# Self-attention of a decoder kernel: the softmax exponentials are divided by their sums on GpSimd ahead of the transposing, in place of dividing the output of the value matmuls

## The chip, the cores and the metric

The kernel runs on one core of a Trainium2 chip. The metric is the device time of one execution in microseconds; lower is better. The core's engines are TensorE (PE in the profile; its weight loads are listed as PEld), VectorE (DVE), ScalarE (ACT), GpSimd (POOL) and SyncE (SP, which issues DMAs here).

## The reference, cut to what matters

The whole program is a two-layer decoder; only the first layer's self-attention changes. It has 2 sequences of 1024 tokens, 16 heads of 64 columns, a relative-position bias, and computes, for each head,

```
scores = q @ k.T * 64**-0.5 + bias[q - k]     # 1024 x 1024
p      = exp(scores - max) / sum(exp(scores - max))
out    = p @ v                                # 1024 x 64
```

Dividing each row of the exponentials by its sum, or dividing the matching row of `exp @ v`, gives the same result up to rounding.

## The kernel before, in words

`self_attention` is written by hand, one instruction stream for each engine, with semaphores between them. A **block** is a pair of heads of one sequence (16 blocks). A block has 8 **iterations**, one for each 128 queries: n runs from 0 to 127. An iteration has two **stages**, one for each head of the pair, numbered st = 2n and 2n+1. I call them the first and the second stage of the iteration. Two iterations make a **group** g of 256 queries (64 groups), whose outputs leave together.

What one stage does, in order of the data:

1. PE `scores` (L578) makes 128 x 1024 scores in two PSUM banks; both stages of the iteration come out of one set of 12 matmuls.
2. DVE `biased` (L730) adds the bias strip, writes 128 x 1024 values to `sm` (a ring of 4 slots) and their extreme to `mn`.
3. ACT `exps` (L663) takes the exponentials in place and puts the row sums in `rsum`.
4. PE `transposed` (L591) waits for `exps` and transposes the eight 128 x 128 pieces into two PSUM banks, which ACT (L668) and DVE (L737), both called `emptied`, copy to `pT`.
5. PE `values` (L606) multiplies the transposed exponentials of a whole group by V, half of it in each iteration of the next group, into one half of bank 6 (64 output columns of each head on the partitions, 256 queries along the bank).

The division runs once a group: DVE `inverted` (L742) takes the reciprocals of 4 columns of sums; PE (L613), behind the second half of `values`, spreads them with 4 small matmuls against the identity into the other half of bank 6; ACT `spread_inverse` (L674) copies that half to `inv`; DVE `normed` (L748) multiplies it with the outputs into `o`; SP stores `o` (L553).

GpSimd has no work in this part of the program. `project` (L629, L634, L637) are the projections for the block after this one, one unit at the end of each iteration n < 120: in each run of 8 iterations four units for k and q, then four for v. The last 8 iterations have none. `split` prepares weights, 7 times.

The order of the work on each engine is the order of the code. On PE, iteration n is: scores(n+1), transposed(n, 0), half of values, transposed(n, 1), project.

Of the kernel before, what the change touches and what calls it, by code (L numbers as in the profile page):

```python
# [24 lines left out]
ALU = mybir.AluOpType  # L25
ACT = mybir.ActivationFunctionType
AX = mybir.AxisListType

P = 128
# [453 lines left out]
def self_attention(nc, A, S, K, psum):  # L483
# [6 lines left out]
    with ExitStack() as ctx:  # L490
# [14 lines left out]
        sm = sb("sm", [P, RING, T])  # L505
        mn, rsum = sb("mn", [P, SUMS]), sb("rsum", [P, SUMS])
        pT = sb("pT", [P, 2, 2, KT, GQ])
        inv = sb("inv", [P, GQ])
        o = sb("o", [P, 2, GQ])


# [22 lines left out]
        with turn(nc, sig) as block:  # L534
# [29 lines left out]
            @block.tensor  # L564
            def _(pe):
                def scores(n):
                    _, b, qt = tiles[n]
                    if n % KT == 0:
                        pe.wait_ge(sig("proj_out"), NU * (n // KT) + 4)
                    if n:  # L570
                        pe.wait_ge(sig("biased"), 2 * n)
                    q = slice(qt * P, (qt + 1) * P)
                    for c in range(2):
                        k = slice(c * CH, (c + 1) * CH)
                        for i, (qq, kk) in enumerate(((QH, KH), (QL, KH), (QH, KL))):
                            for hl in range(2):
                                rows = slice(hl * DH, (hl + 1) * DH)
                                last = pe.matmul(scores_banks(hl)[:, c, :], qq[rows, b, q], kk[rows, b, k],  # L578
                                                 start=i == 0, stop=i == 2)
                                if c == 1 and i == 2:  # L580
                                    last.then_inc(sig("scores"), 1)

                def transposed(n, hl):
                    st = 2 * n + hl
                    pe.wait_ge(sig("exps"), st + 1)
                    for j, emptied in enumerate(("pT_act", "pT_dve")):
                        if st:
                            pe.wait_ge(sig(emptied), st)
                        for k in range(4):
                            kt = 4 * j + k  # L590
                            last = pe.transpose(psum[:, 4 + j, k * P:(k + 1) * P], sm[:, st % RING, kt * P:(kt + 1) * P], ident[:, :])  # L591
                        last.then_inc(sig("p_ps"), 1)

                def values(g, half):

                    _, b, _ = tiles[2 * g]
                    if half == 0:
                        pe.wait_ge(sig("pT_act"), 4 * (g + 1))
                        pe.wait_ge(sig("pT_dve"), 4 * (g + 1))
                        pe.wait_ge(sig("proj_out"), NU * (2 * g // KT + 1))  # L600
                        if g:
                            pe.wait_ge(sig("o_out"), g)
                    for kt in range(half * KT // 2, (half + 1) * KT // 2):
                        for hl in range(2):
                            rows = slice(hl * DH, (hl + 1) * DH)
                            pe.matmul(bank_o[rows, 0:GQ], V[:, b, kt, rows], pT[:, g % 2, hl, kt, :],  # L606
                                      start=kt == 0, stop=kt == KT - 1)
                    if half:
                        pe.wait_ge(sig("inverse"), g + 1)
                        for t in range(2):  # L610
                            for hl in range(2):
                                at = (4 * g + 2 * t + hl) % SUMS
                                last = pe.matmul(bank_o[hl * DH:(hl + 1) * DH, GQ + t * P:GQ + (t + 1) * P],  # L613
                                                 rsum[:, at:at + 1].broadcast_to([P, DH]), ident[:, :], start=True, stop=True)
                        last.then_inc(sig("o_ps"), 1)

                def project(u):
                    pair, b, what, c = units[u]
                    bank, W = unit_bank(u), Ws[pair % 2]
                    if u >= NU:  # L620
                        pe.wait_ge(sig("proj_out"), u)
                    if u % (2 * NU) == 0 and pair:
                        pe.wait_ge(sig("w_lo"), pair)
                    terms = passes(KC)
                    tok = slice(b * T + c * CH, b * T + (c + 1) * CH)
                    if what in "qk":
                        col = slice(0, P) if what == "q" else slice(P, 2 * P)
                        for i, (ws, hs, k) in enumerate(terms):
                            last = pe.matmul(bank, W[:, ws, k, col], hT[hs][:, k, tok], start=i == 0, stop=i == len(terms) - 1)  # L629
                    else:  # L630
                        for t in range(2):
                            tile = slice(b * T + (2 * c + t) * P, b * T + (2 * c + t + 1) * P)
                            for k in range(KC):
                                pe.matmul(bank[:, t * 2 * P:(t + 1) * 2 * P].rearrange("p (s n) -> p s n", s=2), hT[0][:, k, tile],  # L634
                                          W[:, :, k, 2 * P:3 * P], start=k == 0, stop=False)
                            for k in range(KC):
                                last = pe.matmul(bank[:, t * 2 * P:t * 2 * P + P], hT[1][:, k, tile], W[:, 0, k, 2 * P:3 * P],  # L637
                                                 start=False, stop=k == KC - 1)
                    last.then_inc(sig("proj_ps"), 1)

                for u in range(NU):
                    project(u)
                scores(0)
                for n in range(NI):
                    if n + 1 < NI:
                        scores(n + 1)
                    transposed(n, 0)
                    if n > 1:
                        values(n // 2 - 1, n % 2)
                    transposed(n, 1)  # L650
                    if NU + n < len(units):
                        project(NU + n)
                values(NG - 1, 0)
                values(NG - 1, 1)

            @block.scalar
            def _(a):
                def exps(st):
                    a.wait_ge(sig("biased"), st + 1)
                    at = st % SUMS  # L660
                    if st >= SUMS:
                        a.wait_ge(sig("o_ps"), st // 4 - 2)
                    a.activation(sm[:, st % RING, :], sm[:, st % RING, :], ACT.Exp, scale=-1.0,  # L663
                                 bias=mn[:, at:at + 1], accum_out=rsum[:, at:at + 1]).then_inc(sig("exps"), 1)

# [1 line left out]
                    a.wait_ge(sig("p_ps"), 2 * st + 1)  # L667
                    a.activation(probs(st, 0), psum[:, 4, :].rearrange("p (k q) -> p k q", k=4), ACT.Copy).then_inc(sig("pT_act"), 1)  # L668

                def spread_inverse(g):  # L670
                    a.wait_ge(sig("o_ps"), g + 1)
                    if g:
                        a.wait_ge(sig("o_out"), g)
                    a.activation(inv[:, :], bank_o[:, GQ:2 * GQ], ACT.Copy).then_inc(sig("inv_out"), 1)  # L674

                def project(u):

# [24 lines left out]
                exps(1)  # L702
                for n in range(NI):
                    if n % 2 == 0 and n > 2:
                        spread_inverse(n // 2 - 2)
                    emptied(2 * n)
                    if n + 1 < NI:
                        exps(2 * n + 2)
# [4 lines left out]
                        project(NU + n)  # L713
                    if n % (2 * KT) == 2 and n // (2 * KT) + 1 < HP:
                        split(n // (2 * KT) + 1)
                spread_inverse(NG - 2)
                spread_inverse(NG - 1)

            @block.vector
            def _(v):  # L720
# [15 lines left out]
                    v.wait_ge(sig("p_ps"), 2 * st + 2)  # L736
                    v.tensor_copy(probs(st, 1), psum[:, 5, :].rearrange("p (k q) -> p k q", k=4)).then_inc(sig("pT_dve"), 1)  # L737

                def inverted(g):
                    v.wait_ge(sig("exps"), 4 * (g + 1))  # L740
                    part = rsum[:, 4 * g % SUMS:4 * g % SUMS + 4]
                    v.reciprocal(part, part).then_inc(sig("inverse"), 1)  # L742

                def normed(g):
                    v.wait_ge(sig("inv_out"), g + 1)
                    if g >= 2:
                        v.wait_ge(sig(f"st{g % 2}"), 16 * (g // 2))
                    v.tensor_tensor(o[:, g % 2, :], bank_o[:, 0:GQ], inv[:, :], ALU.mult).then_inc(sig("o_out"), 1)  # L748

                def project(u):  # L750

# [21 lines left out]
                    project(u)  # L773
                biased(0)
                biased(1)
                for n in range(NI):
                    if n % 2 == 0 and n > 2:
                        normed(n // 2 - 2)
                    if n and NU + n - 1 < len(units):
                        project(NU + n - 1)  # L780
                    if n + 1 < NI:
# [2 lines left out]
                    if n + 1 < NI:  # L784
                        biased(2 * n + 3)
                    emptied(2 * n + 1)
                    if n % 2:
                        inverted(n // 2)
                    if n % (2 * KT) == 3 and n // (2 * KT) + 1 < HP:
                        split(n // (2 * KT) + 1)  # L790
                normed(NG - 2)
                normed(NG - 1)


def start(nc, have, rows, weights, zeros=None):
# [1503 lines left out]
```

## Time and profile before

| | us |
|---|---|
| median of 3 runs (2507.12 to 2510.59) | 2510.52 |
| the profiled execution | 2507.76 |
| its span in the profile | 2506.0 |
| PE busy over the span | 2126.9 |
| DVE busy | 1527.2 |
| ACT busy | 1034.9 |
| POOL busy | 608.1 |

The self-attention loop lies between about 60 and 935 us of the span. Busy time of PE overlaps its own weight loads, and ends of matmuls are modelled, so the spacing of starts tells more than the durations. A row of a timeline gives the start, the duration, the engine, the line, the operation, its tiles and, in brackets, the idle time of the engine before it and what ended it.

### The profile page before, as it was taken

The numbers are of one execution on the slowest core, as the hardware profiler recorded it, in microseconds if no ns is written. First come the engines' busy times: TensorE is split into PE (matmuls) and PEld (weight loads), VectorE is DVE, ScalarE is ACT, GpSimd is POOL, SyncE is SP. The second block draws the span as 40 slices with busy tenths as digits, with TensorE's granted clock in tenths as the row PEclk, the third lists the DMA queues.
The fourth block names the chain that finished last, engine by engine and source line by source line (L and its number), as shares of the span: only waits on it lengthen the run. The fifth ranks groups of instructions, "written<-read, shape, count | busy, mean of one in ns | idle before, by whom it ended". The sixth has DMA issues, their size and how long they took to land. (4 is left out here: it accounts for less than half of the span.)

```text
span 2506.0 us, 48610 instructions
## 1 busy us (share of the span) xinstructions
PE 2126.9 (85%) x19484; PEld 1756.7 (70%) x19484; DVE 1527.2 (61%) x3236; ACT 1034.9 (41%) x2036; POOL 608.1 (24%) x596
## 2 busy tenths in 40 slices
PE   5999999999999985788876488999658989866885
PEld 4777777777777764676765488888648888865673
DVE  5666666666666651689897455554445454434885
ACT  3666666566665650333432232332223332222442
POOL 1000000000000001466666223323222333323552
PEclk8999999999999997899987699999879999988997
DMA  6001101010110004021100210000021000003000
GB/s 233 14 16 43 43 16 43 16 49 12 47 43 10 12 14 169 27 70 36 36 18 9 97 48 10 10 14 10 5 110 44 15 14 27 10 10 110 10 9 18
DMA packets 59968, 96.79 MB, mean 39 GB/s; under 512 B 7720, under 2 KB 50480, under 8 KB 57392
## 3 DMA queue, kind: packets, MB, share of 16 engines
q1 hardware_dynamic: 52608, 69.49, 8.6%
q10 hardware_dynamic: 7136, 24.19, 2.5%
q8 instruction: 156, 2.56, 0.4%
q14 instruction: 68, 0.56, 0.1%
HBM read 70.45 MB, written 23.20 MB: 37 GB/s over the span
## 5 line engine op out<-in xcount | busy, mean ns | idle before, releaser
L730 DVE CUSTOM_DVE_ANT_0 a_sm<-psum,a_strip 128x1024 f32<-128x1024 f32 x256 | 311.8, 1218 | 34.6 <-PE psum L578 34.4
L663 ACT ACTIVATE a_sm<-a_sm,a_mn 128x1024 f32<-128x1024 f32 x256 | 293.4, 1146 | 29.7 <-DVE a_mn L730 29.6
L591 PE MATMUL psum<-ident,a_sm 128*128 128x128 f32 x2048 | 280.0, 280 | 1.1 <-ACT a_pT L668 1.0
L591 PEld LDWEIGHTS psum<-ident,a_sm 128*128 128x128 f32 x2048 | 219.5, 141 | 83.9 <-issue 58.5
L668 ACT ACTIVATE a_pT<-psum 128x512 f32<-128x512 f32 x256 | 152.9, 597 | 303.5 <-PE psum L591 303.5
L737 DVE COPY a_pT<-psum 128x512 f32<-128x512 f32 x256 | 176.3, 689 | 131.5 <-PE psum L591 131.5
L606 PE MATMUL psum<-a_pT,a_V 128*64 128x256 f32 x2048 | 249.0, 385 | 1.3 <-DVE a_o L748 1.3
L1130 POOL TENSOR_TENSOR b_x<-b_x,b_bo_a 128x512 f32<-128x512 f32 x8 | 10.2, 1280 | 937.6 <-POOLq L798 937.6
L606 PEld LDWEIGHTS psum<-a_pT,a_V 128*64 128x64 f32 x2048 | 136.2, 136 | 77.5 <-issue 22.3
L578 PE MATMUL psum<-a_KH,a_QH 64*128 64x512 f32 x512 | 115.1, 445 | 2.5 <-DVE a_mn L730 2.5
L1020 PE MATMUL psum<-b_w,b_act_hi 128*128 128x256 f32 x256 | 64.7, 337 | 56.3 <-POOL b_act_lo L1118 56.3
L1126 POOL TENSOR_TENSOR b_gs<-b_gate,b_sg 128x512 f32<-128x512 f32 x64 | 96.7, 1510 | 28.5 <-ACT b_sg L1042 27.9
L578 PE MATMUL psum<-a_KL,a_QH 64*128 64x512 f32 x512 | 102.4, 395 | 0.0
L578 PE MATMUL psum<-a_KH,a_QL 64*128 64x512 f32 x512 | 101.7, 392 | 0.0
L225 PE MATMUL psum<-sa_eT,sa_wqkv 128*128 128x256 f32 x768 | 94.5, 283 | 2.8 <-DVE sa_eT L1719 2.7
L225 PE MATMUL psum<-la_eT,la_wqkv 128*128 128x256 f32 x768 | 95.1, 284 | 1.7 <-DVE la_eT L1719 1.7
L225 PEld LDWEIGHTS psum<-sa_eT,sa_wqkv 128*128 128x128 f32 x768 | 92.9, 192 | 3.5 <-DVE sa_eT L1719 3.4
L225 PEld LDWEIGHTS psum<-la_eT,la_wqkv 128*128 128x128 f32 x768 | 93.4, 193 | 2.5 <-DVE la_eT L1719 2.3
L1118 POOL TENSOR_TENSOR b_act_lo<-b_act,b_act_hi 128x512 fp32r<-128x512 f32 x64 | 83.3, 1302 | 48.2 <-ACT b_act_hi L1049 48.2
L1020 PEld LDWEIGHTS psum<-b_w,b_act_hi 128*128 128x128 f32 x256 | 44.9, 213 | 69.9 <-POOL b_act_lo L1118 69.1
L629 PE MATMUL psum<-a_hT_hi,a_W 128*128 128x512 f32 x256 | 76.5, 421 | 12.2 <-PEq L72 12.2
L206 PE MATMUL psum<-b_wo,b_oT 128*128 128x256 f32 x256 | 58.5, 388 | 24.2 <-PEq L798 24.2
(381 smaller groups left out, 4675.4 us busy)
## 6 DMA issues: line engine op xcount, KB each, us to landing
a_strip<-table SPq DMA_DIRECT2D x16, 960.0 KB, 6.7
oT<-a_o SPq DMA_DIRECT2D x64, 128.0 KB, 1.9
b_oT<-oT SPq DMA_DIRECT2D x8, 1024.0 KB, 5.4
a_raw<-in_a_wqkv SPq DMA_DIRECT2D x7, 384.0 KB, 3.2
s_x<-in_x_rev SPq DMA_DIRECT2D x4, 512.0 KB, 8.1
vb<-s_zero SPq DMA_DIRECT2D x8, 256.0 KB, 2.9
b_x<-in_x SPq DMA_DIRECT2D x8, 256.0 KB, 5.5
b_vb<-vb SPq DMA_DIRECT2D x8, 256.0 KB, 6.0
```

The lines of the kernel that those rows point to most:

```text
L225: last = pe.matmul(bank[:, i * CP:(i + 1) * CP], weight[:, wp, k, m * P:(m + 1) * P], cols[:, cp, k, :], start=n == 0, stop=n == len(terms ...
L578: last = pe.matmul(scores_banks(hl)[:, c, :], qq[rows, b, q], kk[rows, b, k], start=i == 0, stop=i == 2)
L591: last = pe.transpose(psum[:, 4 + j, k * P:(k + 1) * P], sm[:, st % RING, kt * P:(kt + 1) * P], ident[:, :])
L606: pe.matmul(bank_o[rows, 0:GQ], V[:, b, kt, rows], pT[:, g % 2, hl, kt, :], start=kt == 0, stop=kt == KT - 1)
L629: last = pe.matmul(bank, W[:, ws, k, col], hT[hs][:, k, tok], start=i == 0, stop=i == len(terms) - 1)
L663: a.activation(sm[:, st % RING, :], sm[:, st % RING, :], ACT.Exp, scale=-1.0, bias=mn[:, at:at + 1], accum_out=rsum[:, at:at + 1]).then_in ...
L668: a.activation(probs(st, 0), psum[:, 4, :].rearrange("p (k q) -> p k q", k=4), ACT.Copy).then_inc(sig("pT_act"), 1)
L730: v.tensor_tensor_reduce(out=sm[:, st % RING, :], in0=scores_banks(hl).rearrange("p c n -> p (c n)"), in1=strip[:, pair % 2, hl, qt * P:qt ...
L737: v.tensor_copy(probs(st, 1), psum[:, 5, :].rearrange("p (k q) -> p k q", k=4)).then_inc(sig("pT_dve"), 1)
L1020: last = pe.matmul(bank[:, t * D:(t + 1) * D], half[:, e % 2, k, t * P:(t + 1) * P], w2[:, e, k, :], start=i == 0, stop=i == len(parts) - 1)
L1118: g.tensor_tensor(act_lo[:, e % 2, :, :], act[:, e % 2, :, :], act_hi[:, e % 2, :, :].bitcast(F32), ALU.subtract).then_inc(sig("m_lo"), 1)
L1126: g.tensor_tensor(gs[:, n % ER, :, :], gate[:, n % ER, :, :], sg[:, n % ER, :, :], ALU.mult).then_inc(sig("m_gs"), 1)
```

## The change

The reciprocals are now taken stage by stage (`inverted(st)` on DVE, one column each), GpSimd multiplies the 128 x 1024 exponentials of the stage with them in place, and `transposed` waits for that product (`scaled`) instead of for `exps`. The four spreading matmuls, the tile `inv` and DVE's `normed` are gone; ACT's `stored` copies the finished outputs from bank 6 to `o`. ACT's reuse of a column of `rsum` now waits for `scaled` instead of `o_ps`.

```diff
@@ tensor
                 def transposed(n, hl):
                     st = 2 * n + hl
-                    pe.wait_ge(sig("exps"), st + 1)
+                    pe.wait_ge(sig("scaled"), st + 1)
@@ values(g, half)
                     if half:
-                        pe.wait_ge(sig("inverse"), g + 1)
-                        for t in range(2):
-                            for hl in range(2):
-                                at = (4 * g + 2 * t + hl) % SUMS
-                                last = pe.matmul(bank_o[hl * DH:(hl + 1) * DH, GQ + t * P:GQ + (t + 1) * P],
-                                                 rsum[:, at:at + 1].broadcast_to([P, DH]), ident[:, :], start=True, stop=True)
                         last.then_inc(sig("o_ps"), 1)
@@ scalar
-                        a.wait_ge(sig("o_ps"), st // 4 - 2)
+                        a.wait_ge(sig("scaled"), st - SUMS + 1)
-                def spread_inverse(g):
+                def stored(g):
                     a.wait_ge(sig("o_ps"), g + 1)
-                    if g:
-                        a.wait_ge(sig("o_out"), g)
-                    a.activation(inv[:, :], bank_o[:, GQ:2 * GQ], ACT.Copy).then_inc(sig("inv_out"), 1)
+                    if g >= 2:
+                        a.wait_ge(sig(f"st{g % 2}"), 16 * (g // 2))
+                    a.activation(o[:, g % 2, :], bank_o[:, 0:GQ], ACT.Copy).then_inc(sig("o_out"), 1)
@@ gpsimd (new)
+                for st in range(2 * NI):
+                    at = st % SUMS
+                    g.wait_ge(sig("inverse"), st + 1)
+                    g.tensor_scalar(sm[:, st % RING, :], sm[:, st % RING, :], rsum[:, at:at + 1], None, ALU.mult).then_inc(sig("scaled"), 1)
@@ vector
-                def inverted(g):
-                    v.wait_ge(sig("exps"), 4 * (g + 1))
-                    part = rsum[:, 4 * g % SUMS:4 * g % SUMS + 4]
-                    v.reciprocal(part, part).then_inc(sig("inverse"), 1)
-                def normed(g):
-                    v.wait_ge(sig("inv_out"), g + 1)
-                    if g >= 2:
-                        v.wait_ge(sig(f"st{g % 2}"), 16 * (g // 2))
-                    v.tensor_tensor(o[:, g % 2, :], bank_o[:, 0:GQ], inv[:, :], ALU.mult).then_inc(sig("o_out"), 1)
+                def inverted(st):
+                    v.wait_ge(sig("exps"), st + 1)
+                    at = st % SUMS
+                    v.reciprocal(rsum[:, at:at + 1], rsum[:, at:at + 1]).then_inc(sig("inverse"), 1)
@@ vector, the loop over n
+                inverted(0)
                 for n in range(NI):
-                    if n % 2 == 0 and n > 2:
-                        normed(n // 2 - 2)
+                    inverted(2 * n + 1)
                     if n and NU + n - 1 < len(units):
                         project(NU + n - 1)
                     if n + 1 < NI:
                         biased(2 * n + 2)
                     emptied(2 * n)
                     if n + 1 < NI:
                         biased(2 * n + 3)
                     emptied(2 * n + 1)
-                    if n % 2:
-                        inverted(n // 2)
+                    if n + 1 < NI:
+                        inverted(2 * n + 2)
```

On PE, in the middle of the program where the projections are for v, this stood before: the transposes of a first stage (L591), the second half of values (L606), the spreading matmuls (L613), the transposes of the second stage, then the projection (L634, L637) and the scores of the iteration after next (L578).

```order
299 L591 MATMUL psum<-ident,a_sm 128x128 x8
300 L606 MATMUL psum<-a_pT,a_V 64x256 x8
301 L613 MATMUL psum<-ident,a_rsum 64x128 x4
302 L591 MATMUL psum<-ident,a_sm 128x128 x8
303 L634 MATMUL psum<-a_W1,a_hT_hi 128x256 x2
304 L637 MATMUL psum<-a_W1,a_hT_lo 128x128 x2
305 L634 MATMUL psum<-a_W1,a_hT_hi 128x256 x2
306 L637 MATMUL psum<-a_W1,a_hT_lo 128x128 x2
```

The same place of the change (transposes are L590 there, values L605, the projection L627 and L630):

```order
290 L590 MATMUL psum<-ident,a_sm 128x128 x8
291 L605 MATMUL psum<-a_pT,a_V 64x256 x8
292 L590 MATMUL psum<-ident,a_sm 128x128 x8
293 L627 MATMUL psum<-a_W1,a_hT_hi 128x256 x2
294 L630 MATMUL psum<-a_W1,a_hT_lo 128x128 x2
295 L627 MATMUL psum<-a_W1,a_hT_hi 128x256 x2
296 L630 MATMUL psum<-a_W1,a_hT_lo 128x128 x2
```

Only the four spreading matmuls are gone; nothing else moved on PE. What stands between the transposes of a second stage and those of the next first stage is still one projection and one set of scores.

On DVE, with the semaphores that each row waits for, an iteration's end stood like this before (L730 is `biased`, L737 the copy that empties a bank of transposes, L742 the reciprocal of four columns, L748 `normed`, L764 the second half of a projection):

```order
307 L730 ISA a_sm,a_mn<-psum,a_strip 128x1024 [waits a_ld_strip0,a_scores,a_p_ps]
308 L730 ISA a_mn 128x1
309 L737 COPY a_pT<-psum 128x4x128 [waits a_p_ps]
310 L742 RECIPROCAL a_rsum<-a_rsum 128x4 [waits a_exps]
311 L748 TENSOR_TENSOR a_o<-psum,a_inv 128x256 [waits a_st0,a_inv_out]
312 L764 TENSOR_TENSOR a_V<-a_V,psum 128x256 [waits a_proj_hi]
313 L730 ISA a_sm,a_mn<-psum,a_strip 128x1024 [waits a_scores,a_p_ps]
```

The same place of the change:

```order
312 L730 ISA a_sm,a_mn<-psum,a_strip 128x1024 [waits a_ld_strip0,a_scores,a_p_ps]
313 L730 ISA a_mn 128x1
314 L737 COPY a_pT<-psum 128x4x128 [waits a_p_ps]
315 L742 RECIPROCAL a_rsum<-a_rsum 128x1 [waits a_exps] x2
316 L758 TENSOR_TENSOR a_V<-a_V,psum 128x256 [waits a_proj_hi]
```

The two reciprocals stand side by side: the first is that of the next iteration's first stage, behind the copy that empties the bank of this iteration's second stage; the second is that of the next iteration's second stage. On POOL there are 256 new rows `TENSOR_SCALAR a_sm<-a_sm,a_rsum 128x1024` in a line, each waiting for its reciprocal.

## Rows read from the trace of the kernel before

**Rows 1.** Busy time by engine, 400 to 600 us (PE, PEld, DVE, ACT, POOL; clock, DMA)
```profile
400.00:600.00 200.00, 200.00 (x1604) 147.70 (x1602) 129.68 (x237) 122.07 (x221) 0.00 (x0) 1.00 0.10 35
```

**Rows 2.** Waits, 200 to 800 us: total us, times, longest
```profile
ACT a_pT L668 <- PE psum L591: 211.0, 175, 1.6
...
PEld psum L591 <- issue: 39.6, 131, 0.4
```

**Rows 3.** Timeline, 861 to 876 us, iterations with v projections
```profile
862.26 1.09 PE L591 MATMUL psum<-ident,a_sm 128*128 128x128 f32 x8
...
865.75 1.09 PE L591 MATMUL psum<-ident,a_sm 128*128 128x128 f32 x8
...
868.34 0.58 PEld L613 LDWEIGHTS psum<-ident,a_rsum 128*64 128x64 f32 x8
...
869.09 1.09 PE L591 MATMUL psum<-ident,a_sm 128*128 128x128 f32 x8
...
870.22 0.69 DVE L737 COPY a_pT<-psum 128x512 f32<-128x512 f32 x1 [1.28 <-PE psum L591]
...
870.83 0.17 DVE L742 RECIPROCAL a_rsum<-a_rsum 128x4 f32<-128x4 f32 x1
...
872.58 1.09 PE L591 MATMUL psum<-ident,a_sm 128*128 128x128 f32 x8
...
875.48 0.64 PEld L591 LDWEIGHTS psum<-ident,a_sm 128*128 128x128 f32 x6 [0.39 <-ACT a_sm L663]
```

**Rows 4.** Timeline, 628 to 636 us, an iteration with a q projection
```profile
628.17 1.09 PE L591 MATMUL psum<-ident,a_sm 128*128 128x128 f32 x8
...
632.16 1.09 PE L591 MATMUL psum<-ident,a_sm 128*128 128x128 f32 x8
```

**Rows 5.** Timeline, 911 to 929 us, the last iterations, without projections
```profile
911.61 1.09 PE L591 MATMUL psum<-ident,a_sm 128*128 128x128 f32 x8
...
914.22 1.09 PE L591 MATMUL psum<-ident,a_sm 128*128 128x128 f32 x8
...
923.06 1.09 PE L591 MATMUL psum<-ident,a_sm 128*128 128x128 f32 x8
...
924.50 1.10 PE L591 MATMUL psum<-ident,a_sm 128*128 128x128 f32 x8 [0.34 <-ACT a_pT L668]
```

**Rows 6.** Groups of POOL instructions, other parts: busy us, mean ns, idle before
```profile
L1118 POOL TENSOR_TENSOR b_act_lo<-b_act,b_act_hi 128x512 fp32r<-128x512 f32 x64 | 83.3, 1302 | 48.2 <-ACT b_act_hi L1049 48.2
...
L1646 POOL TENSOR_TENSOR la_pr<-la_pr,la_mx 128x512 f32<-128x512 f32 x16 | 16.8, 1050 | 68.9 <-DVE la_mx L1700 68.9
...
L1165 POOL TENSOR_TENSOR b_pr<-b_pr,b_mx 128x256 f32<-128x256 f32 x8 | 5.0, 625 | 20.4 <-DVE b_mx L1294 20.4
...
L357 POOL MEMSET s_kb<- 128x1024 f32 x1 | 1.0, 951 | 0.0
```

**Rows 7.** Timelines: DVE hands to POOL (2405 us), POOL hands to PE (1133 us)
```profile
2404.97 0.30 DVE L144 BATCH_NORM_AGGREGATE e_yn_mv<-e_yn_st 128x2 f32<-128x6 f32 x2
...
2405.36 0.22 POOL L153 TENSOR_SCALAR e_yn_rs<-e_yn_mv 128x2 f32<-128x2 f32 x1 [5.45 <-DVE e_yn_mv L144]
...
1132.60 1.26 POOL L1118 TENSOR_TENSOR b_act_lo<-b_act,b_act_hi 128x512 fp32r<-128x512 f32 x1
...
1133.92 0.50 PE L1020 MATMUL psum<-b_w,b_act_hi 128*128 128x256 f32 x2 [0.83 <-POOL b_act_lo L1118]
```

**Rows 8.** Timeline, 925 to 935 us, the end of the loop
```profile
930.20 3.67 PE L606 MATMUL psum<-a_pT,a_V 128*64 128x256 f32 x32 [1.26 <-DVE a_o L748]
...
934.35 0.38 ACT L674 ACTIVATE a_inv<-psum 128x256 f32<-128x256 f32 x1 [4.94 <-PE psum L613]
934.76 0.42 DVE L748 TENSOR_TENSOR a_o<-psum,a_inv 128x256 f32<-128x256 f32 x1 [4.71 <-ACT a_inv L674]
```

**Rows 9.** Timeline near 2412 us: a small DVE instruction beside a POOL one
```profile
2411.25 2.06 POOL L2026 TENSOR_TENSOR e_pr<-e_pr,e_total 128x512 f32<-128x512 f32 x2
...
2412.45 0.90 DVE L247 TENSOR_TENSOR e_top_eq<-e_top_eq,rev 128x16 f32<-128x16 f32 x1
```

More of the change, by code:

```diff
@@ L507, in self_attention @@
         pT = sb("pT", [P, 2, 2, KT, GQ])
-        inv = sb("inv", [P, GQ])
         o = sb("o", [P, 2, GQ])
@@ L605, in values @@
                             rows = slice(hl * DH, (hl + 1) * DH)
-                            pe.matmul(bank_o[rows, 0:GQ], V[:, b, kt, rows], pT[:, g % 2, hl, kt, :],
-                                      start=kt == 0, stop=kt == KT - 1)
+                            last = pe.matmul(bank_o[rows, 0:GQ], V[:, b, kt, rows], pT[:, g % 2, hl, kt, :],
+                                             start=kt == 0, stop=kt == KT - 1)
                     if half:
-                        pe.wait_ge(sig("inverse"), g + 1)
-                        for t in range(2):
-                            for hl in range(2):
-                                at = (4 * g + 2 * t + hl) % SUMS
-                                last = pe.matmul(bank_o[hl * DH:(hl + 1) * DH, GQ + t * P:GQ + (t + 1) * P],
-                                                 rsum[:, at:at + 1].broadcast_to([P, DH]), ident[:, :], start=True, stop=True)
                         last.then_inc(sig("o_ps"), 1)
@@ L704, in _ @@
                     if n % 2 == 0 and n > 2:
-                        spread_inverse(n // 2 - 2)
+                        stored(n // 2 - 2)
                     emptied(2 * n)
@@ L715, in _ @@
                         split(n // (2 * KT) + 1)
-                spread_inverse(NG - 2)
-                spread_inverse(NG - 1)
+                stored(NG - 2)
+                stored(NG - 1)
+            @block.gpsimd
+            def _(g):
+                for st in range(2 * NI):
+                    at = st % SUMS
+                    g.wait_ge(sig("inverse"), st + 1)
+                    g.tensor_scalar(sm[:, st % RING, :], sm[:, st % RING, :], rsum[:, at:at + 1], None, ALU.mult).then_inc(sig("scaled"), 1)
             @block.vector
@@ L786, in _ @@
                     emptied(2 * n + 1)
-                    if n % 2:
-                        inverted(n // 2)
+                    if n + 1 < NI:
+                        inverted(2 * n + 2)
                     if n % (2 * KT) == 3 and n // (2 * KT) + 1 < HP:
                         split(n // (2 * KT) + 1)
-                normed(NG - 2)
-                normed(NG - 1)
 def start(nc, have, rows, weights, zeros=None):
```

## The prediction, made before the changed kernel was run

> **What bounds the kernel now.** I read the busy time by stretches first. In the self-attention loop PE has work in all of the 200 us shown, at a granted clock of 1.00 (the 2.4 GHz level), while DVE is busy 65%, ACT 61% and POOL not at all [rows 1]. Then the waits: ACT waits for transposes (211.0 us in 600), and the longest total on PE's weight-load row is "issue", 39.6 us in 131 pieces of at most 0.4 us [rows 2]. These are not semaphore waits. They stand wherever PE goes from one shape of tile to another, and are as long when nothing is late; the 0.39 us before 875.48 [rows 3] that the profile puts down to an `exps` is the same piece, since the exponentials these transposes need were made an iteration earlier. So PE sets the pace, and an engine beside it costs nothing until it makes PE late.
>
> The timeline gives the pace, read from the starts of the transposes (L591). Inside an iteration, from the first stage to the second: 872.58 to 875.48 is 2.90 us with half of the value matmuls between; 865.75 to 869.09 is 3.34 us where the spreading matmuls stand behind the other half [rows 3]. From a second stage to the next first one, where a projection and the scores lie between: 3.49 us with a v unit (862.26 to 865.75, again 869.09 to 872.58) [rows 3], 3.99 us with a k or q unit (628.17 to 632.16) [rows 4], 2.61 us in the last iterations without a unit (911.61 to 914.22), and 1.44 us for the very last, without scores either (923.06 to 924.50) [rows 5].
>
> **What is removed.** The spreading matmuls' loads take 0.58 us [rows 3], but the gain is smaller: behind them the switch to the transposes takes 0.17 us (868.34 + 0.58 to 869.09), behind the values alone it takes 0.39. What the group loses is the difference of the two spacings, 3.34 − 2.90 = 0.44 us. There are 64 groups; 63 lie in the loop: 63 × 0.44 = 27.7 us. The end of the loop gains by its own rows: the last value matmuls started at 930.20 after 1.26 us of waiting for DVE's `normed` [rows 8]. Now ACT's copy frees the bank sooner and the last DVE copy of transposes releases them, which I put 0.5 us earlier. Then ACT started at 934.35 and DVE ended at 935.18; the value matmuls end at 933.87 [rows 8], so a copy of 0.38 us alone could end at 934.3, 0.9 us earlier. Together 1.4 us. Removed in all: 29.1 us.
>
> ACT's `stored` has the length and the place of `spread_inverse`: nothing. It now does the waiting for the store DMA that DVE did, issued two groups before: nothing. DVE loses `normed` (0.42 us a group) and gets four one-column reciprocals for one of four columns (0.17 us), at 65% busy: nothing, except where it lies on the new path below.
>
> **What is added: a longer way from one transpose to the next.** For a first stage the way is now: transposes of the second stage before it start; 1.13 us later (869.09 to 870.22) DVE starts emptying their bank, 0.69 us [rows 3]; then the reciprocal, which in the row of before overlapped that copy's end and ended 0.09 us behind it (870.83 + 0.17 against 870.91) [rows 3]; hand-over from DVE to POOL 0.09 us (2405.27 to 2405.36), POOL's product G, hand-over from POOL to PE 0.06 us (1133.86 to 1133.92) [rows 7]. The sum is 2.06 + G. Behind this reciprocal nothing else waits; what is queued behind POOL's wait is only the next product. PE waits where 2.06 + G is over the spacing above. Free are G up to 1.43 us with a v unit (60 iterations), 1.93 with a k or q unit (60), 0.55 without (6), and nothing for the very last: 1.44 − 2.06 = −0.62.
>
> The second stage has more time. Its reciprocal is at the head of DVE's iteration, where DVE waits for ACT's part of the projection anyway, and its transposes are at least 2.9 us behind the first stage's. Two products in a row end 2.00 + 2G after the transposes before, and are wanted 3.49 + 2.90 = 6.39 after: free up to G = 2.2. POOL's own load of 2G in some 6.8 us is no bound. The ring of `sm` is released by the transposes as before.
>
> **The price of G.** No POOL instruction of 1024 columns with one tensor input is in the trace. Below it stands a fill of 128 x 1024: 0.95 us [rows 6], which writes as much and reads nothing. Above: a product of 128 x 512 with a factor repeated along the row, 1.05 us, with 0.625 for 256 columns, so 1.66 ns a column and 1.90 us for 1024; and above that the product of two full inputs, 1.30 us for 512 columns, doubled 2.6 us [rows 6]. A small `tensor_scalar` takes 0.22 us [rows 7]. A second operand that is repeated already makes the product cheaper than a full one, so the time goes by what is read; the new instruction reads one tensor and one column. I take 1.1 us, near the fill: the fill's rate for 1024 columns (0.85 us without its fixed part of about 0.1) plus 0.22 fixed.
>
> The Trainium skill (GPSIMD Engine Reference, § 4.1 Engine selection) says that two-input elementwise work is about twice as slow there as on VectorE and one-input work runs about at line rate. The same page's § 3.1 speaks against the change: its best case for a plain loop is 1.8 cycles an element at 1.2 GHz. An estimate from that figure is 1.54 us, and the sum by it would be 14.7 us of waiting, so 14 us gained and not 24. No row here shows either.
>
> With G = 1.1: v units 0, k and q units 0, 6 × 0.55 = 3.3, the very last 1.1 + 0.62 = 1.7: 5.0 us of new waits. Sum: −29.1 + 5.0 = −24.1. The profiled execution of 2507.8 would be 2483.7. The median of the runs shown is 2.8 above it; from it 2510.5 − 24.1 = **2486 us**.
>
> **Does POOL disturb DVE, or DVE POOL?** A DVE instruction with two SBUF inputs and 16 columns took 0.90 us where its like takes 0.17, while POOL multiplied [rows 9]. In the loop only `split` has two inputs from SBUF, 7 times. All the rest of DVE's large work there reads PSUM. If a `split` and a product block each other for 1 us, a q iteration has 1.93 − 1.1 = 0.8 us to spare: under 1 us in all 7.
> The Trainium skill (SBUF — State Buffer, on the pair of ports that VectorE and GpSimd share) says the same: two SBUF inputs contend with a GpSimd instruction that reads SBUF, one does not; the row agrees. By this rule `biased`, with one input in PSUM, goes on untouched.
>
> **Rivals.**
> - *POOL needs 1.5 us* (a loop with more steps than the fill). Waits: 60 × 0.07 + 6 × 0.95 + 2.1 = 12.0; time −17.1: 2493. For it: one scalar is fetched for each instruction, and a multiply is more than a fill. Chance 13%.
> - *POOL needs 1.9 us*, as for the factor repeated along the row, which is the nearest operation in kind. Then every v iteration waits 0.47 us (28.2), the last ones 8.1 and 2.5: 38.8 us against 29.1, +9.7: 2520, slower. This is the case on the other side. It turns at G = 1.76, from 60(G − 1.43) + 6(G − 0.55) + (G + 0.62) = 29.1; every 0.1 us more in the reciprocal or the hand-overs counts like 0.1 us of G. Against it: one tensor is read, not two. Chance 17%.
> - *POOL needs 2.5 us*, as for two full inputs. v iterations wait 1.1 (64 us), k and q ones 0.6 (34), the end 15: +84, so 2595. Chance 7%.
> - *The change removes nothing*, because PE waits for something else in the place of the spreading matmuls. The 2.90 us iterations have the same other work in the same order, so I see nothing; it would be 5 us slower, 2516. Chance 3%.
>
> **How the numbers follow.** My forecast, G from 0.95 to 1.25, has 60%; its own range is 2481 (no waits at all) to 2490. A measurement of this kernel tells about 0.2%, 5 us, from no change. Faster by more than that needs G under 1.68: the forecast, the 1.5 case: 73%. Within it: G from 1.68 to 1.83, or nothing removed and little added: 6%. Slower: 21%. Eight in ten must take in the 1.9 us case: 2480 to 2522; out of it are the 2.5 us case and little else.
>
> **What would show it.** POOL's new rows have a mean of about 1.1 us. Transposes of second stages come 2.90 us after those of first stages in every iteration. The 3.49 and 3.99 us spacings stand unchanged, and that of 2.61 grows to about 3.2. PE's waits for POOL come to 5 us, all behind 880 us. If instead PE waits for POOL in iterations with v units, G or a hand-over is longer than I took it, and the spacing minus 2.06 tells how long. The prediction is wrong above all if G is over 1.7 us.

## The result, and the profile after

The changed kernel takes 2652.35 us (median of 4 runs, 2646.25 to 2654.32), the kernel before 2508.82 in the same runs: ratio 1.0562, 95% interval 1.0545 to 1.0578. It is 143.5 us slower, where 24 us less was forecast. The profiled execution took 2654.32 us, its span is 2652.5.

First the new instruction, in the view of one line: minimum, median and maximum of its duration in ns, then who waited for it.

```profile
L717 POOL TENSOR_SCALAR a_sm<-a_sm,a_rsum x256: 2838/2844/3474, 60.5 to 1061.7; 128x1024 f32<-128x1024 f32 x128
...
  PEld psum L590: 255.2, 252
  PE psum L590: 151.9, 129
```

GpSimd needs 2.84 us for a product that the forecast priced at 1.1. Busy time between 400 and 600 us (columns as in [rows 1]):

```profile
400.00:600.00 200.00, 172.01 (x1305) 123.21 (x1306) 118.11 (x232) 104.20 (x194) 146.08 (x52) 1.00 0.09 31
```

PE issued 1604 matmuls in this stretch before, now 1305; no engine is busy all the time, GpSimd 73%. The waits between 200 and 800 us (total us, times, longest) say what took PE's time. Before, PE's side had "issue" [rows 2] and, behind it, this one, with no piece over 0.4 us:

```profile
PEld psum L591 <- ACT a_sm L663: 16.5, 43, 0.4
```

With the change it is:

```profile
POOL a_sm L717 <- DVE a_rsum L742: 163.2, 77, 2.1
PEld psum L590 <- POOL a_sm L717: 147.6, 153, 1.9
...
PE psum L590 <- POOL a_sm L717: 84.8, 77, 1.4
```

PE waits for GpSimd, and GpSimd, though it is the slow one, waits 2.1 us in each of the 77 iterations for a reciprocal. An engine that is waited for and itself waits is not the bound by its load. The two sit on one ring: PE's transposes, DVE's copy and reciprocal, GpSimd's product, and PE's next transposes, each released by the one before. One turn of it, from the timeline (start, duration):

```profile
505.14 1.09 PE L590 MATMUL psum<-ident,a_sm 128*128 128x128 f32 x8
...
506.27 0.69 DVE L737 COPY a_pT<-psum 128x512 f32<-128x512 f32 x1 [1.07 <-PE psum L590]
...
506.88 0.15 DVE L742 RECIPROCAL a_rsum<-a_rsum 128x1 f32<-128x1 f32 x1
...
507.13 5.67 POOL L717 TENSOR_SCALAR a_sm<-a_sm,a_rsum 128x1024 f32<-128x1024 f32 x2 [2.12 <-DVE a_rsum L742]
...
510.03 1.09 PE L590 MATMUL psum<-ident,a_sm 128*128 128x128 f32 x8 [0.80 <-POOL a_sm L717]
...
512.93 1.09 PE L590 MATMUL psum<-ident,a_sm 128*128 128x128 f32 x8
```

The way is the one that the prediction added up: copy 1.13 us after the transposes, reciprocal, product, transposes. From the second stage's transposes to the next first ones it is 4.89 us (505.14 to 510.03; 4.88 in most iterations), where [rows 3] had 3.49 and [rows 4] 3.99; from the first to the second it is 2.90 (510.03 to 512.93), as forecast, in all but the first two iterations and four of the last six. v, k and q iterations are alike now, 7.79 us each: PE's own work no longer shows.

At the end of the loop something more appears. These are PE's weight loads in an iteration without projections, and then the busy time of 5 us there (PE, PEld, DVE, ACT, POOL; clock):

```profile
1035.14 0.86 PEld L590 LDWEIGHTS psum<-ident,a_sm 128*128 128x128 f32 x8 [2.64 <-POOL a_sm L717]
1036.26 0.30 PEld L605 LDWEIGHTS psum<-a_pT,a_V 128*64 128x64 f32 x4 [0.27 <-issue]
1036.74 0.24 PEld L605 LDWEIGHTS psum<-a_pT,a_V 128*64 128x64 f32 x2 [0.19 <-issue]
...
1039.67 0.42 PEld L590 LDWEIGHTS psum<-ident,a_sm 128*128 128x128 f32 x4 [0.56 <-issue]
```

```profile
1035.00:1040.00 5.00, 4.86 (x27) 2.91 (x28) 1.83 (x3) 1.73 (x3) 2.90 (x2) 0.66 0.00 0
```

Behind a wait of 2.6 us the granted clock is 0.66 over these 5 us, a mean of the 2.4 GHz level and the 1.2 GHz level. 1035.14 to 1039.67 is 4.53 us for what takes 2.90 at the higher level. It happens in four of the last six iterations; the other two follow waits of the same length and take 2.90.

### The profile page after: what moved, and what is told of

Same layout as the page of the kernel before. It is cut to its first block and busy times, and to the rows that moved or that the text cites. A ratio compares the mean times of both kernels' runs of the same rounds, so it can differ in the third digit from the quotient of the medians.

```text
span 2652.5 us, 47907 instructions
## 1 busy us (share of the span) xinstructions
PE 2125.7 (80%) x18972; PEld 1735.7 (65%) x18972; DVE 1549.8 (58%) x3364; ACT 1021.0 (38%) x2036; POOL 1336.7 (50%) x852
## 3 DMA queue, kind: packets, MB, share of 16 engines
q8 instruction: 152, 2.49, 0.4%
## 5 line engine op out<-in xcount | busy, mean ns | idle before, releaser
L717 POOL TENSOR_SCALAR a_sm<-a_sm,a_rsum 128x1024 f32<-128x1024 f32 x256 | 729.6, 2862 | 314.8 <-DVE a_rsum L742 314.8
L590 PE MATMUL psum<-ident,a_sm 128*128 128x128 f32 x2048 | 281.4, 281 | 151.9 <-POOL a_sm L717 151.9
L590 PEld LDWEIGHTS psum<-ident,a_sm 128*128 128x128 f32 x2048 | 220.8, 141 | 257.3 <-POOL a_sm L717 255.2
L730 DVE CUSTOM_DVE_ANT_0 a_sm<-psum,a_strip 128x1024 f32<-128x1024 f32 x256 | 312.3, 1220 | 59.5 <-PE psum L577 59.5
L737 DVE COPY a_pT<-psum 128x512 f32<-128x512 f32 x256 | 177.1, 692 | 262.5 <-PE psum L590 262.5
L605 PE MATMUL psum<-a_pT,a_V 128*64 128x256 f32 x2048 | 255.1, 392 | 0.8 <-DVE a_pT L737 0.8
L605 PEld LDWEIGHTS psum<-a_pT,a_V 128*64 128x64 f32 x2048 | 138.8, 139 | 80.3 <-issue 25.8
L742 DVE RECIPROCAL a_rsum<-a_rsum 128x1 f32<-128x1 f32 x256 | 40.5, 158 | 67.9 <-ACT a_sm L656 67.8
```

The lines of the kernel that those rows point to most:

```text
L605: last = pe.matmul(bank_o[rows, 0:GQ], V[:, b, kt, rows], pT[:, g % 2, hl, kt, :], start=kt == 0, stop=kt == KT - 1)
L717: g.tensor_scalar(sm[:, st % RING, :], sm[:, st % RING, :], rsum[:, at:at + 1], None, ALU.mult).then_inc(sig("scaled"), 1)
L730: v.tensor_tensor_reduce(out=sm[:, st % RING, :], in0=scores_banks(hl).rearrange("p c n -> p (c n)"), in1=strip[:, pair % 2, hl, qt * P:qt ...
```

## The experiments

Each is the changed kernel with one edit, or with two where it says so. Times are medians; ratios are to the kernel before, run on the same chip. In all of them I read the same two things: the product's median, and the spacing from the second stage's transposes to the next first ones.

**The removal alone.** GpSimd's stream and all calls of `inverted` are left out, `transposed` waits for `exps`, and ACT no longer waits for `scaled` before it reuses a column of `rsum`; the outputs are not divided by the sums. The edit, shortened (`...` between places):

```diff
-                    pe.wait_ge(sig("scaled"), st + 1)
+                    pe.wait_ge(sig("exps"), st + 1)
...
-                    if st >= SUMS:
-                        a.wait_ge(sig("scaled"), st - SUMS + 1)
...
-            @block.gpsimd   (and its whole loop)
...
-                inverted(0)
                 for n in range(NI):
-                    inverted(2 * n + 1)
...
-                    if n + 1 < NI:
-                        inverted(2 * n + 2)
```

> The changed kernel without the reciprocals and without GpSimd's product: the transposes wait for the exponentials as before, and the outputs are not divided by the sums. It holds the removal alone. Theory (the removal gives 0.44 us a group and 1.4 us at the end, and nothing else waits): spacings of 2.90 us inside every iteration, 3.49, 4.0 and 2.61 us between iterations, and 29 us less than before, ratio 0.988. Rival (part of the lost time is not GpSimd's wait but comes with the removal itself, such as a lower granted clock or a later copy of the outputs): less than 20 us gained.

Measured: 2479.06 us, ratio 0.9877 (0.9858 to 0.9895). The timeline of PE:

```profile
500.30 1.09 PE L590 MATMUL psum<-ident,a_sm 128*128 128x128 f32 x8
504.30 1.09 PE L590 MATMUL psum<-ident,a_sm 128*128 128x128 f32 x8
507.20 1.09 PE L590 MATMUL psum<-ident,a_sm 128*128 128x128 f32 x8
511.22 1.09 PE L590 MATMUL psum<-ident,a_sm 128*128 128x128 f32 x8
514.12 1.09 PE L590 MATMUL psum<-ident,a_sm 128*128 128x128 f32 x8
517.61 1.09 PE L590 MATMUL psum<-ident,a_sm 128*128 128x128 f32 x8
```

2.90 us inside both iterations, 4.0 and 3.49 between. From the first transposes of the loop to the last it is 835.7 us where the kernel before had 863.4 (64.46 to 927.84): 27.7 us less, the number of the prediction. From there to the end of the last copy is 6.03 us against 7.34: 1.3 less, forecast 1.4. The whole gain that was forecast is there when nothing is added. The rival falls.

**The reciprocal earlier.**

```diff
                         biased(2 * n + 3)
+                        inverted(2 * n + 2)
                     emptied(2 * n + 1)
-                    if n + 1 < NI:
-                        inverted(2 * n + 2)
```

> The changed kernel with one reciprocal moved: that of the next iteration's first stage stands ahead of the DVE copy that empties the second bank, not behind it. The product then starts about 0.2 us after the transposes of the second stage start, not 2.0 us. Theory (the wait is the chain copy, reciprocal, product of 2.84 us, transposes, and GpSimd's 5.7 us of work an iteration still fits into 6.4 us): no waits with k, q or v units, 0.2 to 0.4 us an iteration in the last 8, so 22 to 29 us under before, ratio about 0.99. Rival (GpSimd is the bound by its load, or its products get longer as it works beside more of DVE's work): products over 3 us or PE waiting in all iterations, and a time above that of before.

Measured: 2491.31 us, ratio 0.9923 (0.9904 to 0.9942), products 2.85 us as before. This moves one instruction of 0.16 us and takes back 161 us, with GpSimd as slow as ever. It is 18.5 us under before, where 22 to 29 were expected. Timeline, without projections (near the end):

```profile
889.35 0.16 DVE L742 RECIPROCAL a_rsum<-a_rsum 128x1 f32<-128x1 f32 x1
889.37 1.09 PE L590 MATMUL psum<-ident,a_sm 128*128 128x128 f32 x8
889.60 5.67 POOL L717 TENSOR_SCALAR a_sm<-a_sm,a_rsum 128x1024 f32<-128x1024 f32 x2 [0.36 <-DVE a_rsum L742]
...
892.51 1.09 PE L590 MATMUL psum<-ident,a_sm 128*128 128x128 f32 x8 [0.46 <-POOL a_sm L717]
```

The product now starts 0.23 us after the transposes, not 2.0: 0.23 + 2.84 + 0.06 = 3.13, and 889.37 to 892.51 is 3.14. With projections the spacings are those of before, 3.49 and 4.0, but for the first two and one of 3.70. What is lost against the removal alone, 10 us in the loop, lies at its ends: 3.2 us in the first two iterations, 5.0 in the spacings without projections (0.5 us each where 0.2 to 0.4 was expected, and 1.7 at the very last), and 1.6 in the last iteration, which takes 4.53 us instead of 2.90 at a granted clock of 0.63. GpSimd's load (5.7 us in 6.4 or more) is no bound where there are projections, and its products are no longer than before: the rival falls.

**The factor repeated along the row.**

Here `slot` stands for `sm[:, st % RING, :]`:

```diff
-g.tensor_scalar(slot, slot, rsum[:, at:at + 1], None, ALU.mult)
+g.tensor_tensor(slot, slot, rsum[:, at:at + 1].broadcast_to([P, T]), ALU.mult)
```

> The changed kernel with GpSimd's tensor_scalar written as tensor_tensor with the column of factors repeated along the row; the same values. Theory (the form sets the price, and the 1.66 ns a column of the trace of before holds up to 1024 columns): product 1.9 us, from second to first transposes 2.06 + 1.9 = 3.96 us where 3.49 was, k and q iterations unchanged: 10 to 14 us over before, ratio about 1.005. Rival (1024 columns in place of exponentials just written cost what they cost, whatever the form): product about 2.8 us and the time of the changed kernel, 2650.

Measured: 2521.96 us, ratio 1.0046 (1.0024 to 1.0068). Product 1.89 us (1.90 was worked out from [rows 6]), spacing 3.92. The same values at the same place cost a third less in another form, and the time is that of the prediction's 1.9 us rival, 2520.

**Half the columns.** The product covers `sm[:, slot, 0:512]`; the other half is not divided.

> The changed kernel with a product over the first 512 of the 1024 columns; the rest is not divided. Theory (the price is by columns, and the chain of 2.06 us and the product sets the wait): product 1.45 to 1.55 us, from second to first transposes 3.55 us with v units, 4.0 with k and q units as before, PE waiting only in the last iterations: 15 to 18 us under before. Rival (most of the 2.84 us is fixed, a cost of reading the scalar through a pointer): product over 2 us and a time above that of before.

Measured: 2498.27 us (2491.72 to 2508.01, 10 runs), ratio 0.9956 (0.9941 to 0.9970), so about 11 us gained where 15 to 18 were expected; the prediction's sum gives 12 for a product of 1.57 us. The product takes 1.57 us, where 1.45 to 1.55 was expected. If the price is a straight line between the two widths, a column costs (2.844 − 1.567) / 512 = 2.49 ns and 0.3 us is fixed. The spacing with v units is 3.60. So most of the price goes by columns, and a product only 0.14 us over the free 1.43 already costs 0.11 us in each v iteration.

**Both remedies.** The early reciprocal and the repeated factor.

> Both edits at once: the reciprocal of the next first stage ahead of the DVE copy, and the product as tensor_tensor with the repeated factor (1.89 us). Theory (from second to first transposes 0.23 + 1.89 + 0.06 = 2.2 us, less than every spacing of before but the very last): no waits, spacings as in the run with the removal alone, ratio 0.988, 2480 us, about 11 us under the version with the early reciprocal alone. Rival (a busy GpSimd costs something in itself, by shared reads with VectorE): over 5 us above the run with the removal alone.

Measured: 2483.33 us, ratio 0.9880 (0.9862 to 0.9898); spacings 3.49, 4.0, 2.61, none stretched but the very last (2.39). GpSimd at work 58% of the loop's time (256 × 1.89 of 837 us) beside DVE and ACT costs nothing that shows: the loop takes 836.6 us against 835.7 with the removal alone, and the 0.9 is the very last spacing.

What remained was why `tensor_scalar` is so dear. Four runs vary what GpSimd does and nothing else.

**A constant factor** (0.001 in the instruction; no division).

> The changed kernel with a constant in the instruction (0.001) in place of the column of factors, so the rows are not divided by their sums. If reading the factor through a pointer is what makes the product slow: under 2.0 us and a time near 2520 or less. If tensor_scalar itself is slow: 2.84 us again and 2650.

Measured: product 2.77 us, spacing 4.80, 2638.64 us (one run). The pointer costs 0.07 us, the rest is the instruction's.

**A copy** (`g.tensor_copy` of the slot onto itself; no division).

> The changed kernel with GpSimd copying each slot onto itself (one input, no factor), so the outputs are not divided. If one read and one write a column go at the rate of the fill, as the prediction took it: 1.0 to 1.1 us, PE waits only in the last iterations, and the time that was forecast for the change, about 2484 (ratio 0.990). If a column that is read and written costs what it costs in tensor_scalar: 2.8 us and 2650. The chain of 2.03 us and the product should give the spacing in either case.

Measured: 1.04 us, 2485.85 us, ratio 0.9889 (0.9866 to 0.9911). Reading and writing 1024 columns in place goes at almost the rate of the fill in [rows 6], 0.95. In the last iterations the spacing is 3.05:

```profile
885.88 1.09 PE L590 MATMUL psum<-ident,a_sm 128*128 128x128 f32 x8 [0.36 <-POOL a_sm L717]
888.78 1.09 PE L590 MATMUL psum<-ident,a_sm 128*128 128x128 f32 x8
891.83 1.09 PE L590 MATMUL psum<-ident,a_sm 128*128 128x128 f32 x8 [0.37 <-POOL a_sm L717]
```

**An addition in place of the multiplication** (0.5 added; no division).

> The changed kernel with GpSimd adding a constant to each slot instead of multiplying by the factors, so the rows are not divided. If the price hangs on the operation (a multiply dearer than an add): well under 2.77 us. If it hangs on the instruction (tensor_scalar, whatever it computes): 2.77 us and about 2640 as with the constant factor.

Measured: 2.77 us, 2640.19 us (one run). Adding costs what multiplying costs.

**Two operations in one instruction** (`tensor_scalar(slot, slot, 0.001, 0.5, mult, add)`; no division).

> The changed kernel with two operations in the one tensor_scalar, times a constant and plus a constant, no division. If tensor_scalar carries a second operation through at every column even where none is asked for: 2.8 us again and about 2640. If the second one is paid for only when it is there: over 3.3 us, and the spacing 2.03 us more than the product.

Both expectations missed, and this was the find: the instruction that does more is faster. The view of the line in this run, and under it in the run with one addition:

```profile
L717 POOL TENSOR_SCALAR a_sm<-a_sm x256: 1042/1055/1686, 60.3 to 898.7; 128x1024 f32<-128x1024 f32 x128
```

```profile
L717 POOL TENSOR_SCALAR a_sm<-a_sm x256: 2764/2770/3404, 60.8 to 1050.8; 128x1024 f32<-128x1024 f32 x128
```

1.06 us with two operations, 2.77 with one, for the same 1024 columns; 2489.32 us (one run).

**The changed kernel with a second operation that does nothing.** Whole computation.

```diff
-rsum[:, at:at + 1], None, ALU.mult)
+rsum[:, at:at + 1], 0.0, ALU.mult, ALU.add)
```

> The changed kernel, whole computation, with one edit: GpSimd's tensor_scalar multiplies by the factor and then adds 0.0, two operations in place of one. If the one-operation form is what is slow (two_operations took 1.05 us with constants, and a pointer cost 0.07 us more): product 1.1 us, spacing 3.49 with v units, 3.1 in the last iterations, and the time that was forecast for the change, 2484 to 2488, ratio 0.990. If a factor read through a pointer brings the slow form back: 2.8 us and 2650.

Measured: 2483.55 us, ratio 0.9888 (0.9869 to 0.9907). The rival, that a factor read through a pointer brings the slow form back, falls.

```profile
L717 POOL TENSOR_SCALAR a_sm<-a_sm,a_rsum x256: 1112/1123/1752, 60.4 to 900.7; 128x1024 f32<-128x1024 f32 x128
```

The product takes 1.12 us, the price that the prediction had put on it, and the time is 2.5 us under the predicted 2486. The spacings are 3.49 and 4.0, and 3.16 in the last iterations (forecast about 3.2).

**The same with the early reciprocal.**

> The same with the reciprocal of the next first stage ahead of the DVE copy as well. Theory: the last iterations' waits go too (7 spacings of 3.1 back to 2.61, and 1 us at the very last), 4 to 5 us under the other, ratio 0.988, the same as with the removal alone. Rival (nothing was left to wait for): the same time as the other.

Measured: 2481.23 us, ratio 0.9876 (0.9859 to 0.9894). The last iterations are back at 2.61 us, the very last at 1.63. The loop is 4.9 us shorter than in the run before (4 to 5 expected), but the times differ by only 2.3 us and the intervals overlap. It is as fast as the kernel that leaves the division out, and the lowest time of all whole kernels here.

| run | product us | spacing with v units, us | time, us | ratio |
|---|---|---|---|---|
| the change | 2.84 | 4.88 | 2652.4 | 1.0562 |
| repeated factor | 1.89 | 3.92 | 2522.0 | 1.0046 |
| half the columns (other half not divided) | 1.57 | 3.60 | 2498.3 | 0.9956 |
| reciprocal early | 2.85 | 3.49 | 2491.3 | 0.9923 |
| second operation | 1.12 | 3.49 | 2483.6 | 0.9888 |
| early and repeated | 1.89 | 3.49 | 2483.3 | 0.9880 |
| early and second operation | 1.12 | 3.49 | 2481.2 | 0.9876 |
| no division | none | 3.49 | 2479.1 | 0.9877 |

Where the wait shows (the first three rows), spacing minus product is 2.04, 2.03 and 2.03 us: one chain, and the product is the only part of it that changed.

## Why the prediction was wrong

**The step that failed** is "The price of G": "I take 1.1 us, near the fill". It is 2.84 us. The bounds failed with it: the prediction held that "the time goes by what is read", from a fill, a product with a repeated factor and a product of two full inputs, and so took 2.6 us, twice the two-input row of 512 columns, as the top. An instruction with one tensor input costs more than that. None of these rows is of the form that the change uses; the `tensor_scalar` that the prediction had [rows 7] has 2 columns (0.22 us) and says nothing of the price of a column.

The working around G held:

- **The removal**: 27.7 us in the loop and 1.4 at its end were forecast; the removal alone gave 27.7 and 1.3.
- **The chain**: 2.06 + G forecast, 2.03 to 2.04 + product measured at three products. With G = 2.84 the prediction's own sum gives 60 × 1.41 + 60 × 0.91 + 6 × 2.29 + 3.46 = 156 us of waits.
- **What it left out**: measured from the first transposes of the loop to the last, the change has 1003.6 us and the removal alone 835.7, 167.9 us of waits. The 156 are in it, less 3 (the chain is 2.04 us and not 2.06, and the usual spacing with k and q units is 4.01, not the 3.99 of the one I read). The other 14 are: `split` 7 × 0.63 us (next point), 7.3 us from the lower clock in four of the last iterations, and 2.6 in the first two, where the second stage's transposes come 2.7 to 2.8 us after the first's and not 1.4.
- **Contention**: "under 1 us in all 7" holds only as long as q iterations have time to spare. With the product of 1.12 us they have: beside a `split` it takes 1.75 us and no spacing grows. With the product of 2.84 us they have none: beside a `split` it takes 3.47 us, and the spacing there is 5.51 instead of 4.88.
- **Second stages** have the time they were given: 2.90 us in all but the first two iterations and the four at the lower clock, though G = 2.84 is over the 2.2 that I called free. That bound was reckoned at the old spacing; when the first stage comes late, the second has 4.89 + 2.90 = 7.79 us and needs 2.00 + 2 × 2.84 = 7.7. By the same sums (4.96 + G against 2.00 + 2G) this would be the next wait for G over 2.96, an estimate that no run tests.

On the span the loop's end moved by 137.9 us: the first load of the next part was issued at 939.31, now at 1077.19. The remaining 8.6 us of the profiled execution lie behind the self-attention, in instructions that the change doesn't touch. That part takes 462 us before at a mean granted clock of 0.85, 472 at 0.83 with the change, and also 469 at 0.84 with the removal alone, which is a faster kernel. With the repeated factor, which is slower than before in the loop, it takes 462 again. So it varies from one kernel to another, and not with what the change adds or removes; what sets it stays open.

**The rivals.** The direction was wrong because one term had the wrong size, not because of the mechanism: the rival "POOL needs 2.5 us" had the mechanism and most of the price (2595 us; it is 2652) with a chance of 7%, and even this highest of the prices considered was too low. The chance of 17% for 1.9 us fits a kernel that was not the one tried, the repeated factor. The 60% were a price that exists, 1.12 us, for this same product written with two operations.

**The two rules of the Trainium skill.** The Trainium skill (GPSIMD Engine Reference, § 4.1 Engine selection) says that one-input work there is roughly at line rate. The copy (1.04 us) and the two-operation form (1.06 and 1.12) agree, the one-operation `tensor_scalar` (2.77 and 2.84) does not, and here the measurement decides. The 1.8 cycles of the Trainium skill (the same page, § 3.1), an estimate of 1.54 us for 1024 columns, fit none of them.

The Trainium skill (SBUF — State Buffer, § Who interferes with whom) says that a VectorE instruction with two SBUF inputs contends with a GpSimd one that reads SBUF, and that one with at most one SBUF input, outside the 2-port modes, does not. The second half agrees: beside everything else of DVE the product of the change is 2838 to 2859 ns long. The first half agrees where `split`, which reads two SBUF inputs, starts first: a product that starts 0.17 us behind it takes 3.47 us. Where the product starts first, it depends on the product's form. With the reciprocal early and the factor repeated, `split` starts 1.3 us into the product and takes 1.41 us instead of 0.95; with the reciprocal early alone it starts 1.3 us into a one-operation `tensor_scalar`, and neither is longer than alone, all 7 times (`split` 946 to 948 ns, product 2845 to 2847). No run here shows why. The lines of `split`, early alone and then early and repeated:

```profile
L763 DVE TENSOR_TENSOR a_W<-a_raw,a_W x7: 946/948/948, 89.3 to 727.9; 128x768 fp32r<-128x768 f32 x7
```

```profile
L763 DVE TENSOR_TENSOR a_W<-a_raw,a_W x7: 1407/1408/1409, 86.0 to 724.4; 128x768 fp32r<-128x768 f32 x7
```

What stays open is why GpSimd's one-operation form is slower than its two-operation form. It isn't the pointer (0.07 us), the operation (add as multiply), working in place (the copy is in place too) or mainly a fixed cost (1.57 us for half the columns). That these are two code paths of different quality is a guess; no run here looks inside.

## What to carry to other kernels

Price a new instruction by a row of the same form, not by one that moves the same bytes. If there is no such row, the forecast is the spread of forms, and here it reached from 1.0 to 2.8 us for one read and one write a column. And work out, as a formula with the unknown in it, at what price the change turns; here 1.76 us did, and one measured number would have settled the sign.

When a slow engine waits for others and they for it, the lost time can be won back at any point of that ring. The reciprocal that GpSimd waited for stood behind a copy that it didn't need; moving it ahead of the copy gave back 161 us with the product as slow as ever.

## What the runs showed of the hardware that I had not expected

- GpSimd's `tensor_scalar` on 128 x 1024 float32 takes 2.77 us with one operation and a constant, whether add or multiply, 2.84 with a factor read through a pointer, and 1.06 and 1.12 us with a second operation added. One operation on 512 columns takes 1.57. `tensor_copy` of 1024 columns takes 1.04, `tensor_tensor` with a repeated factor 1.89.
- Waits of PE's weight loads of 2.6 us in each iteration of 7.8 (2.2 us on PE itself) were followed by the 1.2 GHz level in three of the six iterations that had them, and so was one of 4.0 us in the very last iteration (granted clock 0.66 from 1035 to 1040 us, 4.53 us for 2.90 us of work), while waits of up to 1.9 us in each left the granted clock at 1.00 from 200 to 800 us.
- A single longer wait could be enough, and the length of the wait alone doesn't decide: the very last iteration fell to a granted clock of 0.63 (about 4.5 us for 2.90) behind waits of PE of 1.98 us (two operations), 2.04 (reciprocal early), 2.51 (half the columns) and 2.83 (repeated factor), and stayed at 1.00 behind 1.96 (the copy) and 2.07 (second operation added). What decides between them stays open.
- A DVE instruction with two SBUF inputs (`split`, 0.95 us alone) lengthened GpSimd's product by 0.63 us when it had started 0.17 us before it. Started 1.3 us behind GpSimd's, it was itself lengthened to 1.41 us beside `tensor_tensor` and not at all beside the one-operation `tensor_scalar`.
